# Graph attention: windows merged item by item, replaced by scans over each partition's own run of edges

## The reference

```python
h = jnp.maximum(_layernorm(x, axis=-1), 0.0)          # x: 12500 x 128
h = (h @ W_node.T).reshape(num_nodes, H, HD)          # H = 4, HD = 32
e = (edge_features @ W_edge.T).reshape(num_edges, H, HD)   # edge_features: 412500 x 64
att_in = jnp.concatenate([h[src], h[tgt], e], axis=-1)
att = jnp.sum(att_in * a, axis=-1)                    # one logit per edge and head
att = jnp.where(att > 0, att, 0.2 * att)
m = jnp.maximum(jax.ops.segment_max(att, tgt, num_segments=num_nodes), 0.0)
ex = jnp.exp(att - m[tgt])
deg = jax.ops.segment_sum(ones, tgt, num_segments=num_nodes)
denom = segment_sum(ex, tgt) + (num_edges - deg)[:, None] * jnp.exp(-m)
h_prime = segment_sum((ex / denom[tgt])[:, :, None] * h[src], tgt)
return x + h_prime
```

## Time and profile before

| | |
|---|---|
| timed executions (3) | 4969.78, 4975.58, 4982.64 us; median 4975.58 |
| the profiled execution, span | 6376.5 us |
| of it busy: PE, DVE, ACT, POOL | 59%, 41%, 19%, 52% |
| rows gathered | 3224 indirect DMAs of 128 rows |
| moved | 506.25 MB, mean 79 GB/s |

### The profile page before, as it was taken

One profiled execution on the slowest core, in us unless ns is written; L12 is line 12 of the kernel. 1 busy time (PEld: TensorE's weight loads), 2 busy tenths in 40 slices (PEclk: granted clock), 3 DMA queues, 4 the chain that ended last, 5 costly groups with the idle time before them and its releaser, 6 DMA issues.

```text
span 6376.5 us, 88250 instructions
## 1 busy us (share of the span) xinstructions
PE 3777.9 (59%) x24835; PEld 3479.1 (55%) x24835; DVE 2605.6 (41%) x9904; ACT 1215.2 (19%) x3468; POOL 3285.7 (52%) x3330
## 2 busy tenths in 40 slices
PE   3466566666666666666666666666664555544554
PEld 3356555656655555655556655556654445544454
DVE  4333343333333334343343334334344545544454
ACT  2212121212212122121222212121221111111111
POOL 3644545444454444545445454544445567766763
PEclk7566676676666667666666666667666656666665
DMA  6422222222222222222222222222222222322222
GB/s 126 92 82 79 81 81 79 78 79 82 77 84 78 81 77 81 84 80 79 76 81 83 79 81 80 79 76 81 79 76 63 69 74 74 84 76 68 77 81 57
DMA packets 299939, 506.25 MB, mean 79 GB/s; under 512 B 127979, under 2 KB 169403, under 8 KB 299662
## 3 DMA queue, kind: packets, MB, share of 16 engines
q1 hardware_dynamic: 196750, 287.92, 14.9%
q0 software_dynamic: 103168, 218.10, 13.9%
HBM read 490.01 MB, written 15.75 MB: 79 GB/s over the span
## 4 chain that ended last, share of the span: by engine, by line
another core or an unknown queue 37%; PE 17%; issue 15%; DVE 14%; DVEq 9%; ACT 4%; SPq 1%; POOL 1%; DMA 1%; ACTq 1%; POOLq 0%
PE ps_acc L1043 6%; DVEq L285 5%; PE ps_ef L962 5%; DVE val L882 3%; PE ps_hot L1007 3%; DVE hot_t L767 2%; ACT hot L572 1%; POOL gath L489 1%; DVE acc L789 1%; PE ps_ef L963 1%; ACT hot L573 1%; PE ps_ef L956 1%; SPq L323 1%; DVE u L801 1%
## 5 line engine op out<-in xcount | busy, mean ns | idle before, releaser
L489 POOL DMA_INDIRECT gath<-rows_scratch,idx x3224 | 3222.6, 1000 | 2928.1 <-DVE val L882 1983.5
L1043 PE MATMUL ps_acc<-val,hot 128*128 128x137 f32 x8970 | 1816.6, 383 | 215.3 <-DVE val L882 108.5
L1043 PEld LDWEIGHTS ps_acc<-val,hot 128*128 128x128 f32 x8970 | 1726.5, 284 | 243.3 <-issue 122.1
L1007 PE MATMUL ps_hot<-identb,hot_t 128*128 128x128 bf16 x4485 | 729.7, 260 | 896.6 <-issue 847.9
L1008 PE MATMUL ps_tgt<-tcur,hot_t 128*128 128x12 bf16 x4485 | 645.4, 187 | 825.5 <-issue 823.3
L1007 PEld LDWEIGHTS ps_hot<-identb,hot_t 128*128 128x128 bf16 x4485 | 590.4, 147 | 976.5 <-issue 947.1
L1008 PEld LDWEIGHTS ps_tgt<-tcur,hot_t 128*128 128x128 bf16 x4485 | 592.0, 155 | 900.2 <-issue 899.0
L816 DVE TENSOR_TENSOR_SCAN runs_f<-pens,ps_runs 4x128 f32<-4x128 f32 x345 | 141.1, 409 | 2261.3 <-remote 2213.7
L882 DVE TENSOR_TENSOR val<-gath,weight 128x1664 f32<-128x1664 f32 x345 | 645.1, 1870 | 0.0
L962 PE MATMUL ps_ef<-w_att,efb 128*128 128x8 f32 x2976 | 589.9, 333 | 34.0 <-ACT efb L550 26.3
L962 PEld LDWEIGHTS ps_ef<-w_att,efb 128*128 128x128 f32 x2976 | 566.7, 290 | 49.7 <-ACT efb L550 31.2
(11 more groups left out here) (172 smaller groups left out, 3451.5 us busy)
## 6 DMA issues: line engine op xcount, KB each, us to landing
hot_t<-dst_i_scratch SPq DMA_DIRECT2D x345, 416.0 KB
efb<-in_edge_attr_dram SPq DMA_DIRECT2D x247, 416.0 KB
gath<-rows_scratch,idx POOLq DMA_INDIRECT x3224
rows_scratch<-gath SPq DMA_DIRECT2D x14, 462.0 KB, 6.3
pens<-carry_scratch SPq DMA_DIRECT2D x345, 4.0 KB
att_e<-in_x_dram SPq DMA_DIRECT2D x6, 896.0 KB
out_dram<-att_e SPq DMA_DIRECT2D x6, 896.0 KB
att_e<-dst_f_scratch SPq DMA_DIRECT2D x1, 1860.0 KB
```

Source lines behind the costliest of these rows:

```text
L489: pool.indirect_dma_start(gath[:, k * J + j, :], None, rows[:, :], bass.IndirectOffsetOnAxis(ap=idx[:, half, k, j:j + 1], axis=0)).then_in ...
L1007: tp(hotp[j // 8][:, j % 8 * P:(j % 8 + 1) * P], t, identb[:, :])
L1043: last = mm(ps_acc[:, 0:VC], hot[:, q, j, :], val[:, j, :], start=(j == 0), stop=(j == J - 1))
```

## The change

The merge of chunks and windows is gone. Partition p now owns the 3224 consecutive edges p x 3224 and on, since 128 x 3224 is the padded number of edges. A block is 13 of them on each partition, so there are again 248 blocks and 13 gathers in each, now of 136 floats (544 bytes: 4 heads of 32 features and a one, then 4 source logits). What is done with a block:

- logits: source logits from the gathered row, target logits from `td` (a whole table in SBUF), edge logits from PE. On the target side a node's logits are first scattered in DRAM to the place of the node's first edge, loaded into `td`, and carried on to the node's other edges by scans (`targets`).
- `mcols`, the running maximum of a segment, is a scan over 4 x 14 columns. `D1` and `D2` are the differences to it. ACT makes of `D1` the weights `w_exp`, and of `D2` the factors `A`, one for each of 132 x 14 columns, both in PSUM.
- sums: one product of the 13 gathered rows and the weights (L571), and one scan over 1848 columns (L581) that decays the running sum by `A` and adds the new value. Column 0 of each 14 takes over from the block before (L578).
- ACT copies the state of all 13 edges, 136 floats each, to `R` (L412), and SP stores it, 905 KB a block, to `state_d` in DRAM.

After the last block each node's state is gathered from the place of its last edge: 98 indirect DMAs, 7 to a group, then division, residual and store by groups. Segments that cross from one partition to the next are repaired for at most one node a partition (`fix_*`).

Ahead of the loop, the first and last edge of every node are counted out: ACT counts for each node, over 512 chunk ends, how many chunks lie before it; POOL gathers that chunk of 806 targets, 99 indirect DMAs; VectorE counts within it. Then 98 indirect DMAs scatter the target logits. The layouts of the inputs (x transposed, edge features in pairs of blocks with the feature along the partitions, targets in fp32 and int16, padding) are now prepared before the launch and given to the program as inputs.

The node stage keeps h transposed throughout (`hT`), centres with a product against a constant matrix, and needs no transposes.

The core of the diff:

```diff
-            def gathers(b, half):
-                first = isinstance(b, int) and b == 0
-                pool.wait_ge(idx_ready, b + 1)
-                for k in range(SLOTS):
...
-                        pool.wait_ge(val_done, used)
-                        pool.sem_inc(slots_taken, 1)
-                    for j in range(J):
-                        pool.indirect_dma_start(gath[:, k * J + j, :], None, rows[:, :],
-                                                bass.IndirectOffsetOnAxis(ap=idx[:, half, k, j:j + 1], axis=0)).then_inc(gather_dma[k], 16)
...
+            for k in range(W + 1):
+                if k % 9 == 0:
+                    pool.wait_ge(chunk_ready, k // 9 + 1)
+                if k >= RING:
+                    pool.wait_ge(chunk_used, k - RING + 1)
+                gather(ring[:, k % RING, :], dst16[:, :], chunk_i[:, k:k + 1], chunk_dma[k % RING])
+            rstd_of(0)
+            rstd_of(1)
+            pool.wait_ge(tdst_filled, 64)
+            pool.wait_ge(put_ready, 1)
+            for g in range(STEPS):
+                pool.wait_ge(rows_ready, g + 1)
+                for n in range(NG):
+                    k = g * NG + n
+                    scatter(tdst_d[:, :], put_i[:, k:k + 1], tnode[:, k, :], scattered)
...
+            def body(it, q):
+                s = q % SLOTS
+                if s == 0:
+                    pool.wait_ge(idx_dma[q // SLOTS], it * 16 + 16)
+                after(pool, val_done, it * UN + q - SLOTS + 1)
+                pool.sem_inc(slots_taken, 1)
+                for j in range(KB):
+                    gather(slots[:, s * KB + j, :], rows[:, :], idx[:, q // SLOTS, s * KB + j:s * KB + j + 1], gather_dma[s])
...
+            for k in range(2):
+                pool.wait_ge(store_dma[k], 16 * (BLOCKS // 2))
+            pool.wait_ge(val_done, BLOCKS)
+            gather(s_first[:, :], state_d[:, :], fe_i[:, 0:1], fix_gather)
+            for g in range(STEPS):
+                if g >= 7:
+                    pool.wait_ge(group_done, g - 6)
+                for n in range(NG):
+                    k = g * NG + n
+                    gather(slots[:, k % 49, :], state_d[:, :], get_i[:, k:k + 1], get_dma[g])
...
-                nc.vector.tensor_copy(vh[:, :, :, HD], weight[:, :, :])
-                nc.vector.tensor_tensor(vh[:, :, :, 0:HD], rows_c[:, :, 0:D].rearrange("p j (h d) -> p j h d", h=H),
-                                        wt.broadcast_to([P, J, H, HD]), ALU.mult).then_inc(val_done, 1)
...
+            def sums(b, k, s, fresh):
+                dve.wait_ge(w_ready, b + 1)
+                v4 = vcols(k)[:, 0:VAL, :].rearrange("p (h v) t -> p h v t", h=H)
+                nc.vector.tensor_tensor(v4[:, :, :, 1:COL],
+                                        slots[:, s * KB:(s + 1) * KB, 0:VAL].rearrange("p t (h v) -> p h v t", h=H),
+                                        w_exp[k].rearrange("p (h a t) -> p h a t", h=H, a=1).broadcast_to([P, H, HB, KB]),
+                                        ALU.mult).then_inc(val_done, 1)
...
+                nc.vector.tensor_tensor_scan(V[:, k, 0:VAL * COL], a_all, V[:, k, 0:VAL * COL], 0.0, ALU.mult, ALU.add).then_inc(scanned, 1)
...
+                nc.scalar.activation(w_exp[v], D1[:, v, :], ACT.Exp).then_inc(w_ready, 1)
...
+                nc.scalar.copy(R[:, k, :, :], vcols(k)[:, :, 1:COL].rearrange("p c t -> p t c")).then_inc(copied, 1)
...
+                sp.dma_start(state_rows[:, ds(b * (KB * ROW), KB * ROW)], R[:, k, :, :].rearrange("p t r -> p (t r)")).then_inc(store_dma[k], 16)
```

More of the change, by code:

```diff
@@ L3, with graph_attention_kernel @@
 from contextlib import ExitStack
-def graph_attention_kernel(nc, x, src, dst, edge_attr, w_node, w_edge, att_vec, out):
+P = 128
+N = 12500
+E = 412500
+D = 128
+H = 4
+HD = 32
+K = 64
+W = 98
+NP = P * W
+T = 3224
+KB = 13
+BLOCKS = T // KB
+PAIRS2 = BLOCKS // 2
+SLOTS = 4
+HB = HD + 1
+VAL = H * HB
+ROW = VAL + H
+COL = KB + 1
+CL = 512
+CE = P * T // CL
+SENTINEL = 16000
+BIG = 2.0 ** 126
+EPS = 1e-5
+NG = 7
+STEPS = W // NG
+UN = 8
+ITERS = BLOCKS // UN
+RING = 8
+PIECES = 8
+PT = T // PIECES
+def graph_attention_kernel(nc, x, x_t, src, dstf, dst16, lasts, ends, first, ea, w_node, w_node_t, a_blk, we2,
+                           ident_c, centre_c, cols_c, out):
     fp32, bf16, i32, i16 = mybir.dt.float32, mybir.dt.bfloat16, mybir.dt.int32, mybir.dt.int16
@@ L290, in spread, with loop @@
[L290 to L297 removed]
+        def loop(eng, body):
+            for q in range(UN):
+                body(0, q)
+            with eng.Fori(1, ITERS) as it:
+                for q in range(UN):
+                    body(it, q)
@@ L423, in _ @@
[L423 to L428 removed]
+            sp.dma_start(last_b[:, :], lasts.broadcast_to([P, CL])).then_inc(loaded_lasts, 16)
@@ new lines, in _, with body @@
+            dve.wait_ge(pen_done, 1)
+            targets(0)
+            dve.drain()
+            def body(it, q):
+                first_block = isinstance(it, int) and q == 0
+                logits(it, q)
+                if isinstance(it, int) and q < PIECES - 1:
+                    targets(q + 1)
+                if not first_block:
+                    sums(it * UN + q - 1, 1 - q % 2, (q - 1) % SLOTS, isinstance(it, int) and q == 1)
+            loop(dve, body)
+            dve.drain()
```

1401 lines of the change are left out of this document (582 added, 819 removed).

## The result

The changed kernel takes 4531.28 us (median of 4, 4519.71 to 4531.99), the kernel before, measured beside it, 4978.66. The ratio is 0.910, 95% interval 0.909 to 0.912: 9% faster. The forecast was 4520 us, in a range of 4390 to 4790.

The account below looks back on a forecast made before the run. The prediction took the kernel before to be bound by POOL's gathers, 704 us of it L882 holding them up. For the changed kernel 285 + 4062 + 166 = 4513, plus 7, gave 4520 us; range 4390 to 4790.

Parts of the forecast that it names:

- the rebuilt 4969 us: Kernel before, timed: start 240.7, 244 chunks x 19.13 = 4668, and 60 behind the last gather; 4975.6 measured.
- Something in the recording costs 1401 us: Profile of the kernel before: span 6376.5 us against median 4975.6, put down to recording slowing PE's bursts.
- The 704 us of stalls by L882: Loop before: L882, with two SBUF operands, holds up POOL's gathers, 704 us of the timed execution.
- my 2.07 us: Gather just ahead of L882 takes 3.02 us, 2.07 more than its neighbours; counted once an item.
- No stall beside L571 and L581: New loop: L571 and L581, one SBUF and one PSUM operand each, were taken not to hold gathers.
- Rival 1: New loop: VectorE's streams L571 and L581 hold gathers despite PSUM, 1513 us, so 6030 us; chance 0.08.
- the prediction's 4265 us: Rebuilt time before if, as the skill infers, two-SBUF-input `tensor_tensor` did not hold gathers: 4969 - 704.
- The loop: New loop: 3224 gathers at 1.26 us, 0.01 of it for short operations, 4062 us.
- What must fit under 16.4 us: Work per block, by engine: VectorE 8.6 us, ACT 3.9, DMA 8.1; POOL sets the pace and never waits.
- Ahead of the loop: Preparation: 12 + 124 chunk gathers + 20 powers + 6 projection + 123 scatters = 285 us.
- Behind the loop: After the last row gather: 27 us, then 124 for 99 state gathers, 16 for the last group; together 166.
- the 7 us added at the end: Sum for the changed kernel: 7 us added to 4513, by which the rebuilt time before fell short.

Follow-up runs that it names:

- experiment 2: Kernel before with 7 of 13 gathers a chunk, sums not the reference's: 3786.11 us, ratio 0.762.
- experiment 5: Kernel before with the carry in another PSUM bank and small tables as uint16, L882's weights still in SBUF: 4966.0 us, ratio 0.9995.
- the fourth group: Last of four groups of runs, each on its own chip; the kernel before took 6429 us in it (6418 to 6485, seven executions).
- Experiment 1: Kernel before with the weights of L882 in PSUM instead of SBUF, carry bank and small tables also changed: 4311.22 us, ratio 0.868.
- experiment 3: Changed kernel with the weights of L571 in SBUF instead of PSUM: 5111.72 us, ratio 1.030 to the kernel before.
- experiment 6: Changed kernel with the decay factors of scan L581 in SBUF instead of PSUM: 5253.74 us, ratio 1.057 to the kernel before.
- experiments 4 and 11: Changed kernel with 7 of 13 gathers a block: 3895.22 us; the same with L412 copying 7 of 13 edge states: 3599.05 us.
- experiment 7: Changed kernel with every block's states stored twice, the second time to another tensor: 4522.08 us.
- experiment 8: Changed kernel with 14 of its 98 scatters before the loop, the other orders not delivered: 4449.78 us.

## Why the prediction came out right, and what in it was wrong

**The bound before** was read rightly, with the wrong reason. The gathers bound it (experiment 2), the rebuilt 4969 us agree with the span of experiment 5, 4967.8. But "Something in the recording costs 1401 us" has fallen. Experiment 5 has its profile from an execution of 4969.75 us, recorded in the same way, and its span is 4967.8, and in the fourth group the kernel before took 6429 us in all seven executions. So the profiled execution of 6376.5 us was of a kind in which this kernel really takes that long, with PE's bursts spread by "issue". What it is that keeps PE waiting there, and what decides when, stays open. Taking the undisturbed durations and rebuilding the time from them was right all the same. That the sum came within 2 us of experiment 5 is partly luck: there a chunk takes 19.26 us instead of 19.13, which makes 244 of them 30 us dearer, while the fifth chunk starts at 235.9 instead of 240.7 and only 35 us follow the start of the last gather instead of 60. The 60 came from the stretched execution. What the changed kernel takes beside a before of 6429 us was not run.

**The 704 us of stalls by L882** measured 634 at L882 itself and 658 by moving its operand (experiments 5 and 1), of 751 in all. I had not named L767, which has 73 of them, and smaller pieces have the rest. The rebuilt sum hid the omission because my 2.07 us were those of a gather held for L882's whole length, while the mean over all L882 is less: 634/345 = 1.84.

**No stall beside L571 and L581**: right, and the reason is shown. With one operand moved to SBUF each of them holds gathers (experiments 3 and 6, 584 and 752 us more by the spans). Rival 1's mechanism thus exists, its condition doesn't hold: "PSUM for one operand may not free the interface that the gathers need" is refuted in both kernels. On the section of the Trainium skill that the prediction cites ("SBUF — State Buffer", Who interferes with whom): its rule on one SBUF input agrees for L882, L571 and L581 (0.94 to 0.97 us beside them); L767 holds gathers with one SBUF tensor, and whether it runs in a two-port mode, which the rule excepts, no run here shows. That `tensor_tensor` isn't seen to hold up descriptor generation can't be carried over to these gathers, as the prediction's 4265 us did: they are held in experiments 3 and 5 and not in 1. Which part of a gather is held is another matter, since a gather also reads its row numbers (`idx`) from SBUF. The products and scans of experiments 3 and 6 hold only gathers that begin beside them, at an early point some 0.8 us before the end, and let pass those that were under way when they began (177 in experiment 3, one of them long, and 118 in experiment 6). L767 holds gathers at a late point too. That fits the section's inference that `tensor_tensor` leaves the making of descriptors alone, and doesn't prove it; no run parts the two.

**The loop**: 4057 us against 4062, 1.2588 us against 1.26. Of the 10 ns that I had added for short stalls, 4 are in the mean gather (954 against 950) and 5 in the gap (305 against 300). Nothing shows that short stalls make them.

**What must fit under 16.4 us** was right in its outcome and wrong in its sizes. L571 takes 3.24 us (forecast 1.92) and L412 3.19 (1.77); L581 with 4.01 (3.98) and L401 with 1.71 were right. Worse, I added up each engine and found 7.8 us of room; the work forms one ring over two engines, 13.8 us long (experiments 4 and 11), so the room was 2.6. "It never waits" came out true by 2.6 us, not by 7.8: here the mechanism was missed and the margin was large enough. PE has 13 small products for each block (3224 in all), not for two. The transfers were no bound (experiment 7).

**Ahead of the loop**: 289.5 against 285, by terms that offset each other. The first chunk gather came at 12.9 (forecast 12). The last ended at 147.0 instead of 136: eight times POOL waited there for VectorE's counts, 7.5 us in all over its usual 0.3, and one gather took 3.80 us. The powers took 16.4 instead of 20; the projection of the first group hid beside them instead of costing 6; 98 scatters at 1.27 took 124 instead of 123. The gather of t_first and the waits for stores, 10 us by the text, were left out of its sum, which would be 295 with them; they took 1.6. That POOL's pace covers the others there was right only in part, as experiment 8 shows.

**Behind the loop**: 171 against 166: 29 us from the last row gather to the first state gather (forecast 27), 123 for the 99 gathers (124), 19 for the last group (16).

**Where the time went.** From experiment 5's trace to that of the changed kernel, the 3224 gathers with their gaps go from 3788.8 + 974.1 = 4763 us to 3076.0 + 982.4 = 4058, -705. What stands outside them goes from 205 to 459, +254. Together -450, and 4967.8 - 4517.7 = 450. The prediction had 704 of stalls gone, 32 of short ones added and 250 uncovered. These three don't make its own forecast: 4969 - 704 + 32 + 250 = 4547, where its sum has 4513. The sum counts some 215 us as uncovered, because it puts 236 outside the gathers in the kernel before, where experiment 5 has 205. The parts of the sum come within 5 us each (start +4.5, loop -5, end +5), and the 7 us added at the end are shown by no run: 4513 against a span of 4517.7. Experiment 1 gave the 658 us back without the rest, and so ends 220 us below the changed kernel. Experiment 3 is the other half of that: the rewritten loop with the product's weights in SBUF takes 5112 us, more than the kernel before. So the rewriting gains nothing without its operands in PSUM.

## What to carry to other kernels

Where indirect DMAs set the pace, look for long VectorE operations with two SBUF operands beside them and move one operand to PSUM: here that alone gave 13%, the rewriting of the merge, PSUM operands included, 9%, and with one of those operands in SBUF again it lost 3 or 6%. Before trusting a long span, compare it with the timed runs, and work with durations and pitches that are undisturbed. Slack is to be counted along the ring of waits over all engines, not engine by engine; halving the work of the bounding engine shows it in one run.

## Unexpected in the hardware

- A gather on POOL that starts inside a long VectorE operation with two SBUF operands ends 0.76 to 0.85 us after that operation (3.72 beside 3.24, 3.54 beside 4.08, 3.01 beside 1.87 us). Beside the scan of experiment 6 those that began up to 0.043 us after it were not held, those from 0.045 us on were. Beside L882 in experiment 5 even the ones that began up to 0.33 us ahead of it are held (239 of the 339); two short operations stand right before it, and whether they are what holds these at first wasn't tried.
- L767, one tensor and a scalar column at 0.4 ns an element, holds gathers too (1.33 us beside 0.65), and still does at 0.7 (1.69 beside 1.21). It does so in two ways: a gather that begins inside it ends some 0.8 us after it, one that is under way when it begins ends 0.12 us after it.
- Transposing fp32 operations run at 1.8 to 1.9 ns an element on VectorE and on ACT, read strided or written strided.
- A power of 49 elements takes 8.20 us on POOL; for 7 it was 1.48, so it isn't quite in proportion (0.17 and 0.21 us an element).
- A scatter takes 0.967 us where a gather takes 0.954.
